# VectorE normalises the first two sequences of a linear-recurrence layer itself, and all engines get a new order

## The reference

```
xn  = layernorm(x)                                   # over the 128 features, no weights
r, k, v = split(xn @ W_rkv + b_rkv, 3)
r   = sigmoid(r);  k = exp(k);  kv = k * v
lam = exp(-exp(nu_log));  gamma = exp(nu_log + gamma_log) - 1
u1  = scan(u1 * lam + kv);  u2 = scan(u2 * lam + k)  # along the 512 steps
s   = ((u1 + gamma*kv) / (u2 + gamma*k + 1e-6) * r) @ W_o + b_o
z   = dequant(quant(xn)) @ dequant(quant(W_ffn)).T + b_ffn
out = x + s * silu(z)
```

## Time and profile before

| | |
|---|---|
| time, median of 3 runs | 120.75 us (120.02 to 122.67) |
| time of the profiled execution | 120.27 us |
| span of the profiled execution, first to last instruction | 118.5 us |
| mean granted TensorE clock | 0.986 of full speed |
| busy: TensorE / VectorE / ScalarE / GpSimd | 109.9 / 107.1 / 102.0 / 100.6 us |
| read and written in HBM | 4.53 MB and 4.19 MB |

### The profile page before, as it was taken

How to read it: one execution, slowest core, us unless ns; L and a number is a source line. 1 busy time by engine, 2 the same in 40 slices (tenths; PEclk the granted TensorE clock), 3 DMA queues, 4 the chain that set the end, 5 groups by cost and what they waited for, 6 DMA issues and landing times.

```text
span 118.5 us, 1729 instructions
## 1 busy us (share of the span) xinstructions
PE 109.9 (93%) x407; PEld 61.1 (52%) x407; DVE 107.1 (90%) x173; ACT 102.0 (86%) x184; POOL 100.6 (85%) x136
## 2 busy tenths in 40 slices
PE   4958999779999999999999999999999999999970
PEld 4945444345456455564564545555556455464450
DVE  0547999999999999999999999999999999998881
ACT  4048599999999999999999999999899999799800
POOL 2289689967999998999998999999999999899600
PEclk9996799999999999999999999999999999999999
DMA  3879950000000201020002020111120211202027
GB/s 70 236 228 401 390 203 0 0 0 3 6 6 0 89 19 69 0 89 0 0 6 89 0 89 0 45 44 55 39 97 0 89 45 44 89 0 89 0 89 266
DMA packets 6025, 8.82 MB, mean 74 GB/s; under 512 B 1536, under 2 KB 1920, under 8 KB 6016
## 3 DMA queue, kind: packets, MB, share of 16 engines
q1 hardware_dynamic: 5040, 8.72, 20.5%
q10 hardware_dynamic: 976, 0.00, 0.4%
HBM read 4.53 MB, written 4.19 MB: 74 GB/s over the span
## 4 chain that ended last, share of the span: by engine, by line
PE 73%; DVE 8%; DMA 6%; POOL 3%; SPq 3%; ACT 2%; issue 2%; DVEq 1%; POOLq 0%
PE taken_ps L1004 30%; PE turned_ps L983 10%; PE so_ps L1060 10%; PE v_ps L1032 9%; PE num_ps L1046 7%; DMA x_all<-in_L_attn_inputs_dram 6%; PE so_ps L1066 5%; DVE stats L458 2%; POOL q L312 2%; PE turned_ps L1060 1%; SPq L233 1%; DVE own_ps L467 1%; DVE x_all L531 1%; ACT xn L744 1%; DVE num_ps L505 1%
## 5 line engine op out<-in xcount | busy, mean ns | idle before, releaser
L1004 PE MATMUL taken_ps<-xnT,wrkv_sb 128*128 128x512 f32 x64 | 33.1, 614 | 0.6 <-ACT xnT L753 0.6
L744 ACT ACTIVATE xn<-x_all,shift,rstd 128x128 f32<-128x128 f32 x48 | 20.1, 489 | 5.6 <-POOL shift L293 5.6
L341 POOL TENSOR_TENSOR mixed<-mixed,den 128x512 f32<-128x512 f32 x16 | 20.6, 1285 | 1.0 <-DVE mixed L520 0.5
L335 POOL TENSOR_TENSOR den<-den,gk 128x512 f32<-128x512 f32 x16 | 20.4, 1285 | 0.7 <-DVE den L496 0.6
L505 DVE TENSOR_TENSOR_SCAN num_ps<-own_ps,kv 128x512 f32<-128x512 f32 x16 | 19.3, 1208 | 0.1
L496 DVE TENSOR_TENSOR_SCAN den<-own_ps,k 128x512 f32<-128x512 f32 x16 | 19.2, 1206 | 0.0
L727 ACT ACT_TABLE_LOAD x14 | 18.0, 1283 | 0.9 <-PEq L1229 0.7
L458 DVE BATCH_NORM_STATS2 stats<-x_all 128x6 f32<-128x256 f32 x32 | 11.8, 418 | 6.3 <-DMA x_all<-in_L_attn_inputs_dram 6.3
L319 POOL TENSOR_TENSOR xd<-q,scale 128x512 f32<-128x512 fp8e4 x16 | 16.9, 1057 | 0.0
L312 POOL TENSOR_TENSOR q<-xn,inv_scale 128x512 fp8e4<-128x512 f32 x16 | 16.9, 1056 | 0.0
L1004 PE MATMUL taken_ps<-xdT,wdT 128*128 128x512 f32 x32 | 16.6, 599 | 0.0
(11 more groups left out here) (71 smaller groups left out, 191.5 us busy)
## 6 DMA issues: line engine op xcount, KB each, us to landing
x_all<-in_L_attn_inputs_dram SPq DMA_DIRECT2D x16, 256.0 KB, 6.7
out_dram<-x_all SPq DMA_DIRECT2D x16, 256.0 KB, 2.0
wrkv_sb<-in_L_attn_W_rkv_dram SPq DMA_DIRECT2D x1, 192.0 KB, 4.1
wf_sb<-in_L_ffn_weight_dram SPq DMA_DIRECT2D x1, 64.0 KB, 6.7
wo_sb<-in_L_attn_W_o_dram SPq DMA_DIRECT2D x1, 64.0 KB, 6.5
cols<-in_L_attn_nu_log_dram ACTq DMA_DIRECT2D x1, 0.5 KB, 3.7
cols<-in_L_attn_gamma_log_dram ACTq DMA_DIRECT2D x1, 0.5 KB, 4.1
cols<-in_L_attn_b_o_dram ACTq DMA_DIRECT2D x1, 0.5 KB, 4.3
```

Of the source, the lines that this page charges most:

```text
L335: nc.gpsimd.tensor_tensor(den[:, n % DEN, :], den[:, n % DEN, :], gk[:, n % KS, :], ALU.add)\
L341: nc.gpsimd.tensor_tensor(mixed[:, n % MIX, :], mixed[:, n % MIX, :], den[:, n % DEN, :], ALU.mult)\
L744: ins = nc.scalar.activation(xn[:, n % XN, j * D:(j + 1) * D], x_all[:, n, j * D:(j + 1) * D], ACT.Identity, bias=shift[:, t:t + 1], scale ...
L1004: nc.tensor.matmul(taken_ps[i % 2][:, :], weights, moving, start=True, stop=True).then_inc(filled, 1)
```

## The change

The arithmetic of the result stays the same. For the sequences 0 and 1 (FIRST = 2) VectorE scales all four tiles itself with one new line, (x - mean) * rstd, taking the mean straight from the statistics. ScalarE and GpSimd no longer normalise these two, and GpSimd no longer computes negmean and shift for their batches. The semaphores of the others count from the third sequence. The run-up has 30 transpositions. The first numerator scan also waits for lam_placed, since it now stands in another place. The lists of TensorE, VectorE, ScalarE and GpSimd are written in a new order from the first steps to the last, and TURNS and TAKEN with them; the helpers `ring`, `quantise(n, m=1)` and so on can take several sequences at once, and every call takes one.

```diff
-    WARM_UP = 32
+    WARM_UP = 30
+    FIRST = 2
...
+        def wait_normalised(engine, n):
+            if n < FIRST:
+                engine.wait_ge(xn_first, n + 1)
+            else:
+                engine.wait_ge(xn_ready, n + 1 - FIRST)
+                if POOL_TILES:
+                    engine.wait_ge(xn_pool, n + 1 - FIRST)
...
             def deviations(b):
...
-                nc.gpsimd.tensor_scalar(negmean[:, lo:hi], stats[:, lo:hi, 1], -1.0, 0.0, ALU.mult, ALU.add)\
-                    .then_inc(negmean_ready, 1)
+                if b >= FIRST:
+                    nc.gpsimd.tensor_scalar(negmean[:, lo:hi], stats[:, lo:hi, 1], -1.0, 0.0, ALU.mult, ALU.add)\
+                        .then_inc(negmean_ready, 1)
...
-                pool.wait_ge(negmean_ready, b + 1)
-                pool.wait_ge(rstd_ready, b + 1)
-                nc.gpsimd.tensor_tensor(shift[:, lo:hi], negmean[:, lo:hi], rstd[:, lo:hi], ALU.mult)\
-                    .then_inc(shift_ready, 1)
+                if b >= FIRST:
+                    pool.wait_ge(negmean_ready, b + 1 - FIRST)
+                    pool.wait_ge(rstd_ready, b + 1)
+                    nc.gpsimd.tensor_tensor(shift[:, lo:hi], negmean[:, lo:hi], rstd[:, lo:hi], ALU.mult)\
+                        .then_inc(shift_ready, 1)
...
         @block.vector
...
+            def normalise(n):
+                dve.wait_ge(stats_done, n + 1)
+                dve.wait_ge(rstd_ready, n + 1)
+                for j in range(TPP):
+                    t = tile(n, j)
+                    ins = nc.vector.tensor_scalar(xn[:, n, j * D:(j + 1) * D], x_all[:, n, j * D:(j + 1) * D],
+                                                  stats[:, t, 1:2], rstd[:, t:t + 1], ALU.subtract, ALU.mult)
+                ins.then_inc(xn_first, 1)
...
             def scan_num(n):
                 if n == 0:
+                    dve.wait_ge(lam_placed, 1)
                     dve.wait_ge(num_armed, 1)
...
             statistics(0)
             statistics(1)
+            normalise(0)
             statistics(2)
+            normalise(1)
             statistics(3)
...
         @block.scalar
...
-            normalise(0)
-            normalise(1)
             copy_xnT(0)
+            copy_xnT(1)
             decays()
-            copy_xnT(1)
             keys(0)
+            keys(1)
             normalise(2)
```

More of the change, by code:

```diff
@@ L224, in tile, with pairs, half, wait_out @@
             return n * TPP + j
+        def pairs(ap):
+            return ap.rearrange("f (p j) -> f p j", j=2)
+        def half(ap, h):
+            return in_time(ap)[:, :, 2 * h:2 * h + 2]
+        def wait_out(engine, n):
+            engine.wait_ge(dve_result, RES_DVE.index(n) + 1)
+        def wait_normalised(engine, n):
[5 more added lines that the diff above has]
+                    engine.wait_ge(xn_pool, n + 1 - FIRST)
         ACT_TILES = [0, 1, 2]
@@ L324, in gamma_k @@
+            def gamma_k(n, m=1):
                 if n == 0:
                     pool.wait_ge(gam_ready, 1)
[L326 to L342, removed]
+                pool.wait_ge(taken_used, taken("k", n + m - 1) + 1)
+                if n + m > KS:
+                    pool.wait_ge(den_ready, n + m - KS)
+                nc.gpsimd.tensor_scalar(ring(gk, n, m), ring(k, n, m), gam[:, 0:1], 0.0, ALU.mult, ALU.add)\
+                    .then_inc(gk_ready, m)
@@ L616, in _ @@
+            receive(1)
             key_values(4)
+            scan_den(2)
+            statistics(13)
+            scan_num(2)
             gating(0)
+            scan_den(3)
+            gamma_kv(2)
+            residual(0)
+            receive(2)
+            key_values(5)
+            statistics(14)
+            gating(1)
             scan_num(3)
-            scan_den(3)
-            residual(0)
+            statistics(15)
             block_maxima(4)
+            scan_den(4)
             receive(3)
-            gating(1)
+            key_values(6)
@@ L624, in _ @@
+            residual(1)
             scan_num(4)
-            residual(1)
-            statistics(12)
-            key_values(5)
-            receive(4)
+            key_values(7)
+            block_maxima(5)
             block_scales(4)
             inverse_scales(4)
+            scan_den(5)
+            receive(4)
+            gating(2)
             scan_num(5)
-            gating(2)
+            residual(2)
             gamma_kv(5)
-            scan_den(4)
-            residual(2)
-            receive(5)
@@ L637, in _ @@
-            key_values(6)
-            scan_den(5)
-            statistics(13)
-            scan_num(6)
-            key_values(7)
-            scan_den(6)
-            block_maxima(5)
-            statistics(14)
-            statistics(15)
-            key_values(8)
-            gating(3)
             block_scales(5)
             inverse_scales(5)
+            receive(5)
+            gating(3)
+            scan_den(6)
+            residual(3)
+            scan_num(6)
+            scan_den(7)
+            block_maxima(6)
@@ L679, in _ @@
             block_scales(7)
             inverse_scales(7)
+            gamma_kv(9)
+            scan_den(10)
+            receive(9)
+            key_values(11)
+            scan_num(10)
+            gating(7)
+            block_maxima(8)
+            key_values(12)
+            receive(10)
+            residual(7)
             scan_num(11)
-            gating(7)
+            scan_den(11)
             gamma_kv(11)
-            key_values(12)
-            residual(7)
-            scan_den(11)
+            block_scales(8)
@@ L889, in _ @@
-            exp_phase()
             keys(7)
             inverse(3)
+            rough_std(5)
+            logarithm(4)
+            copy_xdT(4)
+            inverse(4)
+            keys(8)
+            silu_phase()
+            receptance(7)
+            gates(3)
             normalise(10)
+            normalise(11)
             copy_xdT(5)
-            logarithm(4)
-            copy_xnT(10)
-            keys(8)
+            gates(4)
+            copy_xnT(9)
+            receptance(8)
+            normalise(12)
@@ L897, in _ @@
+            copy_xdT(6)
+            copy_xnT(10)
+            receptance(9)
+            copy_xnT(11)
+            gates(5)
+            exp_phase()
+            keys(9)
             logarithm(5)
-            keys(9)
-            inverse(4)
+            keys(10)
+            inverse(5)
             logarithm(6)
-            keys(10)
-            rough_std(5)
-            inverse(5)
+            normalise(13)
+            copy_xdT(7)
             inverse(6)
+            copy_xnT(12)
+            logarithm(7)
@@ L1130, in _ @@
-            values(7)
-            keys(8)
-            keys(9)
-            values(8)
-            transpose_xn(10)
-            project(3)
-            gamma_kv(6)
-            transpose_xd(6)
+            ffn(4)
+            project(3)
+            receptance(8)
+            transpose_xd(6)
+            untranspose(3)
+            transpose_xn(10)
+            receptance(9)
+            ffn(5)
+            transpose_xn(11)
+            gamma_kv(6)
+            project(4)
+            keys(9)
```

578 lines of the change are left out of this document (275 added, 303 removed), and 16 rows, old and new, of tables (TAKEN, TURNS).

## The result

The changed kernel takes 121.63 us (median of 5 runs, 121.62 to 121.65), the kernel before 120.30 us beside it: ratio 1.0098, interval 1.0065 to 1.0132. It is 1.3 us slower. (The kernel before has one slow run of 122.67 us among its five, which the ratio leaves out.) The forecast was 119.9, with a range up to 121.6. The profiled execution has a span of 119.9 us, where the kernel before has 118.5.

What follows compares the result with a forecast made beforehand. Four engines looked full, with TensorE's gapless chain from 26 us; VectorE was to bind next. VectorE's terms, start -0.1, end -0.6 and middle +0.3, summed to -0.4 us: 119.9 us, range 118.2 to 121.6.

Steps and rivals of the forecast that it cites:

- TensorE's start: First transposition at 7.2 to 7.3 us, 2.2 us earlier; pause after the run-up nearly gone, low clock shrinking with it.
- VectorE, start: VectorE's first steps: 1.6 us of idle time back against 1.5 us for eight added scalings, net -0.1 us.
- my upper price: Eight early VectorE scalings cost 2.05 us if GpSimd's power for sequence 1 holds up the first four.
- the free price: Lower end for VectorE's eight early scalings: 0.13 us each, 1.04 us together, from the output weights' scaling.
- the second rival: Scalings blocked by GpSimd at the start, output weights' scaling up to 0.85 us more: 121.6 us, chance 0.20.
- TensorE ceases to bind: From the second gamma product, TensorE could finish at 110.5 us with 2.7 us of slack; VectorE is late next.
- the idle time after 30 us: Sign that the forecast is right: TensorE shows visible idle time after 30 us; no size given.
- Middle: VectorE, new order everywhere: 0.3 us added to its 0.40 us of idle time, bounds -0.4 and +1.5.
- End: VectorE's last two waits for projections covered (-0.65 us), 0.05 us lost by coming later: -0.6 us.

Runs made afterwards that it cites:

- e1: Changed kernel with gam_diag, wq, wd and the output weights taking their factor from PSUM: 119.53 us, 0.9925 of the kernel before.
- e2: Kernel before with gam_diag, wq, wd and the output weights taking their factor from PSUM: 119.12 us, 0.9923 of the kernel before.
- e4: Kernel before in its old order, but VectorE normalises the first two sequences: median 121.90 us, 1.0135 of the kernel before.

## Why the prediction was wrong

TensorE's start: right in kind. I expected 7.2 to 8.2 us for the first transposition, it is 7.99, and the clock did not drop. But the pause, which was to go all but for a little, stayed at 1.60 us: I had the run-up end at 7.17, and it ended at 6.38. So the clock held without the reason that I gave for it, and why is open.

VectorE, start: the term was mis-sized. The idle time came back as worked out (1.53 us of 1.6). The eight scalings cost 2.04 us from start to next start, where I took 1.5. That is my upper price, 2.05, and it was met by luck: I feared GpSimd's power beside them, which does nothing, and took the free price from the output weights (0.13 to the next start). That row is a scaling by a number; these have two columns and a second operation. The term is +0.5 in place of -0.1.

The constants: this is the step that failed. The sum had no term for them, so it counted them at nothing, and only the second rival had one of them, the output weights at "up to 0.85 more" (0.58 measured). All four together became 1.8 us longer. The rows were there: gam_diag at 0.60 us, ending 0.08 behind GpSimd. A new order moves not only these instructions but everything on GpSimd that they meet. By e1 the stalls cost the changed kernel 2.1 us, by e2 the kernel before 1.2.

The second rival's time, 121.6, was met in part by luck. Its condition held, eight scalings over 1.9 us, but the power of GpSimd did not hold them; wq, wd, gam_diag and the output weights were held.

TensorE ceases to bind: wrong. The second gamma product came at 29.83 in place of 28.6, behind VectorE's scan, which ended at 29.77; three of the constants stand ahead of it and had become 1.2 us longer. TensorE lost its lead in gaps until 41 us, so the idle time after 30 us that I named as a sign came, but as waiting for VectorE and not as slack: from 41 to 92 us it is idle for 0.03 us. The experiments with extra work show slack on neither of the two engines, in either kernel.

Middle: +0.3 of idle time expected, -0.05 measured. End: 0.65 us of waits less were expected; 0.38 went (1.49 to 1.11), since the gating moved behind the last receive waits for its own projection (0.36).

The sum in measured terms: first data 0.12 later, scalings +2.0, constants +1.8, the rest of VectorE's work -0.5, idle time -2.0, together +1.4 us of VectorE, which is the 1.4 us between the two spans.

## What to carry to other kernels

When four engines are full in a fixed order, an earlier start is paid for on the engine that takes the work over, and the added busy time to look for is not only that of the new instructions but that of old ones whose neighbours change. Before an instruction of VectorE with two SBUF inputs, or a scaling from SBUF to SBUF, is moved, look at what GpSimd does there: beside a 128x512 instruction its 0.2 to 0.3 us become up to 1.1 (1.3 for four elements in e4). A factor in PSUM takes the luck out of it, and paid more here (1.2 us in the old order) than the change was forecast to (0.4).

## What was not expected of the hardware

The Trainium skill, SBUF — State Buffer, "Who interferes with whom", has VectorE, in a two-port mode or with two SBUF inputs, and GpSimd exclude each other: the later of the two blocks for the whole of the other's instruction. The 128x512 instructions agree (ends 0.08 to 0.15 us behind GpSimd's). GpSimd's power does not: it runs for 1.06 us on four elements a partition, and VectorE's scalings beside it, the one by a number included, take what they take alone (0.22, 0.28, 0.34). What sets this apart, the size or the power itself, was not tried.

A scaling of 128x128 on VectorE took 0.06 us more with one column in place of a number, and 0.06 more again with a second column and a second operation. And 2.2 us of repeated transpositions made the span 2.5 us longer in one order and 3.4 in the other.
